# Attention with an expert layer: another order of the maxima's products, and loads issued at the start of a round

## The chip, the cores and the metric

One core of a Trainium2 chip. The metric is the device time of one execution in microseconds (us).

## What is computed

The reference, cut to the attention that the change touches (the expert layer that follows is not changed):

```
x = x + attention(layernorm(x), ctx, ctx)        # 4 batches, 1024 positions, 512 features
  qh = (q @ Wq.T), kh = (k @ Wk.T), vh = (v @ Wv.T + bv)     # 16 heads of 32
  scores = einsum('bhsd,bhtd->bhst', qh, kh) / sqrt(32)
  scores[mask: t >= s, except (0, 0)] = -inf
  probs = softmax(scores, axis=-1)
  out = einsum('bhst,bhtd->bhsd', probs, vh) @ Wo.T + bo
x = x + experts(layernorm(x))                     # 32 experts, 4 sets, tokens chosen by a maximum
```

## The kernel before

The kernel runs in three stages: the projections of 8 chunks of 512 positions (to about 290 us), the attention (to about 850 us), then output projection, routing and experts. Queries and keys are split in two parts each and stacked, so that one product over 96 rows is exact enough; a 97th row carries the negated maximum of each query.

The attention has 16 rounds (`NIT`, the variable `it`), one for each batch and group of four heads. The softmax needs the maximum of each query's scores before its exponentials. So there are two kinds of products on TensorE. The **maxima's products** (function `chunk`, line 1538) have queries on the partitions and keys in the columns; 48 of them make one round's maxima: 16 of `FIRST`, of 128 to 512 columns, for the first half of the queries, and 32 of `LATE`, 16 of them with the diagonal (128 to 512 columns) and 16 of 512 columns. The **scores** (function `score`, line 1559) have keys on the partitions; ScalarE turns them into exponentials (line 1450), and `values` and `sums` (lines 1578, 1592) multiply these with the values and add them up. While round `it` makes its scores, the maxima's products of round `it + 1` are put between them. Those of round 0 are put between the products of the projections of chunks 3 to 7, one in each of 48 places.

The twelve steps of a round (`STEPS`) go in six groups of two. TensorE's loop runs for each group: `full_width(it, g)`, then `values` and `sums` of the group. `full_width(it, g)` has eight slots; each ends with a score of the next group, and ahead of it stand as many maxima's products as `SHARE[g]` has for this slot. Which products they are, `FIRST` and then `LATE` say by their order. So three tables set the order on TensorE, and VectorE reads in the same order.

Maxima's products go into a ring of three PSUM banks (`MR = 3`, `reuse`): a product may start when VectorE has read the one three places back. VectorE reads a product with the diagonal by a custom instruction that also adds the mask (line 1313, followed by a readout of its accumulator), a full one by a reduction (line 1316). The scores have a ring of three banks of their own with ScalarE. When the 16 early maxima of the next round are read, TensorE transposes them (`turn`, line 1548, even numbers), ScalarE negates them (line 1428), SyncE copies them into the row of the query stack (`place_row`, line 1085); the 32 late ones follow in slot 2 of group 0 of the next round (odd numbers). A turn takes a place in the ring of three too. The early turn stands at the head of `full_width(it, EARLY_AT)`; `EARLY_AT` is one more than the first group by whose end 16 products have been made, here 2. The early row is needed by the first scores of the next round, made in `full_width(it, 5)`, the late row by those of `full_width(it, 1)`.

Between the products VectorE also inverts the sums of a half (`invert`, ahead of its products of groups 1 and 3), ScalarE copies outputs and sums out of PSUM (`take`), and GpSimd masks exponentials (lines 1193, 1197), adds up those of the full steps (`join`, line 1208, whose result the last `sums` of a round read) and multiplies outputs by the inverses (`divide`).

SyncE's queue has in each round: the late row, the store of the previous round's second half, the early row of the next round, a wait until four of this round's steps are done (`FETCH = 4`), the ten load DMAs of round `it + 2` (`load`: queries, keys, values, 3.5 MB), the store of this round's first half. The operands lie in three slots, so round `it + 2` takes those of round `it - 1`.

Of the kernel before, what the change touches and what calls it, by code (L numbers as in the profile page):

```python
# [19 lines left out]
NCH = T // CH  # L20
# [768 lines left out]
def project_attend_route(nc, a, m, keep):  # L789

    NIT = B * NG
# [6 lines left out]
    NS = len(STEPS)  # L798
    SPAN = [(max(CH * sh, P * j), CH * (sh + 1) - max(CH * sh, P * j)) for sh, j in STEPS]
    TOGETHER = [CH // w if w <= CH // 2 else 1 for _, w in SPAN]  # L800
    UNITS = [HG // n for n in TOGETHER]
    UNIT0 = [sum(UNITS[:k]) for k in range(NS + 1)]
    DIAG = [k for k, (sh, j) in enumerate(STEPS) if P * j >= CH * sh]

    FIRST = [(0, 0), (3, 1), (2, 2), (3, 2), (2, 1), (0, 2), (1, 3), (3, 0), (2, 0), (0, 1), (1, 0), (2, 3), (1, 1),
             (1, 2), (0, 3), (3, 3)]
    LATE = [(2, 5, 0), (1, 4, 1), (2, 7, 0), (0, 7, 0), (3, 5, 1), (3, 6, 1), (0, 5, 0), (3, 6, 0), (2, 7, 1),
# [3 lines left out]
    CHUNKS = [(h, i, 0, (i + 1) * P, True) for h, i in FIRST]  # L811
    EARLY = len(CHUNKS)
    for h, i, diag in LATE:
        CHUNKS.append((h, i, CH, (i + 1) * P - CH, True) if diag else (h, i, 0, CH, False))
    assert len(set(FIRST)) == HG * ST // 2 and len(set(LATE)) == HG * ST
    NC = len(CHUNKS)
# [6 lines left out]
    FULL = [k for k, (sh, j) in enumerate(STEPS) if P * j < CH * sh]  # L823
    JOINS = len(FULL) - 1
    FULL_AFTER = {6: 1, 8: 2, 10: 3}
    FETCH = 4

    INVERSIONS = {1: 1, 3: 0}
    TURN_SLOT = 2

    SHARE = [[1, 2, 0, 1, 1, 2, 1, 0], [0, 2, 0, 2, 1, 2, 1, 1], [4, 0, 1, 1, 1, 1, 0, 2], [1, 0, 0, 1, 0, 2, 2, 1],
             [1, 1, 0, 0, 1, 3, 0, 1], [2, 1, 0, 2, 1, 0, 0, 1]]

    def portions(g, chunks):
        return SHARE[g] if chunks else [0] * (2 * HG)

    PER = [sum(share) for share in SHARE]
    EARLY_AT = 1 + min(g for g in range(len(GROUPS)) if sum(PER[:g + 1]) >= EARLY)
# [14 lines left out]
    with ExitStack() as ctx:  # L853
# [6 lines left out]
        def sem(name):  # L860
            return ctx.enter_context(nc.semaphore(name))
# [101 lines left out]
        q_stored = sem("q_stored")  # L963
# [21 lines left out]
        step_done = sem("step_done")  # L985
# [55 lines left out]
        def fetch_q(eng, it, half, done):  # L1041

            b, g, slot = it // NG, it % NG, it % SLOTS
            for n, part in enumerate((m.q_hi, m.q_hi, m.q_lo)):
                src = part.rearrange("g (h p) (b s) -> b g p h s", p=HD, b=B)[b, g, :, :, half * CH:(half + 1) * CH]
                eng.dma_start(qs[slot][n * HD:(n + 1) * HD, half].bitcast(F32), src).then_inc(done, 16)

        def fetch_k(eng, it, cols, done):

            b, g, slot = it // NG, it % NG, it % SLOTS  # L1050
            for n, part in enumerate((m.k_hi, m.k_lo, m.k_hi)):
                src = part.rearrange("g (h p) (b s) -> b g p h s", p=HD, b=B)[b, g, :, :, cols]
                eng.dma_start(ks[slot][n * HD:(n + 1) * HD, :, cols].bitcast(F32), src).then_inc(done, 16)

        def fetch_v(eng, it):

            src = m.v.rearrange("(b t p) (g n) -> b g p t n", b=B, p=P, g=NG)[it // NG, it % NG]
            eng.dma_start(vt[it % SLOTS][:], src).then_inc(loaded[it % SLOTS], 16)

        def load(eng, it):  # L1060
            done = loaded[it % SLOTS]
            fetch_q(eng, it, 0, done)
            fetch_k(eng, it, slice(0, S), done)
            fetch_q(eng, it, 1, done)
            fetch_v(eng, it)

        with nc.Block() as block:
            @block.sync
            def _(sp):
# [7 lines left out]
                def store(it, half):  # L1077
                    sp.wait_ge(divided, it * 2 + half + 1)
                    sp.dma_start(m.o.rearrange("g p (b s) -> b g p s", b=B)[it // NG, it % NG][:, half * CH:(half + 1) * CH],
                                 o_n[:, half]).then_inc(o_stored[half], 16)  # L1080

                def place_row(turn):
                    it, late = turn // 2, turn % 2
                    sp.wait_ge(m_row_ready, turn + 1)
                    sp.dma_start(qs[it % SLOTS][R:R + 1, late].rearrange("p h s -> p (h s)").bitcast(F32),
                                 m_row[late][:].bitcast(F32)).then_inc(m_placed, 16)
# [60 lines left out]
                for it in range(NIT):  # L1147
                    place_row(2 * it + 1)
                    if it == NIT - 1:
                        sp.wait_ge(o_stored[0], 16 * it)  # L1150
                        sp.wait_ge(o_stored[1], 16 * (it - 1))
                        sp.wait_ge(step_done, it * NS)
                        sp.wait_ge(mx_read, NIT * NC)
                        router.sync_tiles(sp)
                    if it > 0:
                        store(it - 1, 1)
                    if it == NIT - 2:
                        sp.wait_ge(step_done, it * NS)
                        router.sync_weights(sp)
                    if it + 1 < NIT:  # L1160
                        place_row(2 * it + 2)
                    if it + 2 < NIT:
                        sp.wait_ge(step_done, it * NS + FETCH)
                        if it == 0:
                            sp.wait_ge(q_stored, 32 * NCH)
                        load(sp, it + 2)
                    store(it, 0)
                store(NIT - 1, 1)
                router.sync(sp)
# [528 lines left out]
def build(nc, a, m):  # L1698


    with ExitStack() as ctx:
        base = -(-nc.sbuf_base // 64) * 64
        sizes = (("pick", NE * T // P), ("x0", T), ("f1", 2 * NE * F), ("raw1", T), ("bias", E4), ("raw0", T), ("inner", E4 * NGR),
                 ("spare", T), ("wide", NE * NGR), ("x2_in", 3 * 4 * P), ("o_sum", 4 * 4 * P))
        keep = Plan()
        keep.at = {}
        for name, words in sizes:
            keep.at[name] = base
            base += words * 4

        def put(name, shape):
            return nc.alloc_sbuf_tensor_at("kept_" + name, shape, F32, offset=keep.at[name])

        keep.pick_tok = put("pick", [P, T // P, NE])
        keep.x0 = put("x0", [P, T // P, P])
        keep.f1 = put("f1", [P, 2, NE * F])
        keep.raw = [put("raw0", [P, T]), put("raw1", [P, T])]
        keep.bias = put("bias", [P, E4])
        keep.raw_in = ctx.enter_context(nc.semaphore("xn_raw_in"))
        keep.inner = put("inner", [P, E4, NGR])  # L1720
        keep.spare = put("spare", [P, T])
        keep.wide = put("wide", [P, NE * NGR])
        keep.x2_in = put("x2_in", [P, 3, 4, P])
        keep.o_sum = put("o_sum", [P, 4, 4, P])
        project_attend_route(nc, a, m, keep)
# [50 lines left out]
```

## Time and profile before

| | us |
|---|---|
| median of 3 runs | 1200.48 |
| lowest and highest | 1195.95, 1202.35 |
| the profiled execution, its time | 1198.24 |
| its span, first to last instruction | 1196.4 |

| engine | busy us | share of the span |
|---|---|---|
| TensorE, matmuls | 1140.7 | 95% |
| TensorE, weight loads | 781.5 | 65% |
| VectorE | 871.7 | 73% |
| ScalarE | 601.3 | 50% |
| GpSimd | 534.1 | 45% |

The mean granted clock of TensorE is 0.986. A matmul that has started counts as busy even while it waits for room behind another, and its end is modelled, so the busy share of TensorE alone doesn't show what it could save; the distances between starts in the timeline do. Rows below come from this execution; times in them are microseconds from the start of the span.

### The profile page before, as it was taken

To read this page: it belongs to the slowest core of one execution; us is meant where nothing else is said; L and a number is where in the kernel's file an instruction comes from. 1 tells how busy PE (TensorE), PEld (TensorE's weight loads), DVE (VectorE), ACT (ScalarE), POOL (GpSimd) and SP (SyncE) were. 2 spreads that over 40 slices of the span, in tenths; PEclk is the share of its full clock that TensorE was granted. 3 is DMA by queue.
4 is the path that set the end of the run, shared out by engine and by line. 5 is a ranking of instruction groups with operands and counts; after the bars stand their busy time and mean duration, and the time that the engine had idled before them with its cause. 6 is when DMAs were issued, how large, how long until landed. Compare 5 with 4: busy or idle time off the path is not lost. (4 is left out here: it accounts for less than half of the span.)

```text
span 1196.4 us, 29020 instructions
## 1 busy us (share of the span) xinstructions
PE 1140.7 (95%) x11456; PEld 781.5 (65%) x11456; DVE 871.7 (73%) x2202; ACT 601.3 (50%) x1108; POOL 534.1 (45%) x738
## 2 busy tenths in 40 slices
PE   7999999999999999999999999999999997888886
PEld 6787888887555555555555555554588886775664
DVE  7755777773777778777777877775488886766566
ACT  4322222223566666656666656667344444447674
POOL 1000000012666678776666877667765540001343
PEclk9999999999899999999999999999999999999898
DMA  8979887867554445665444566521499976754756
GB/s 290 337 254 300 276 316 247 305 207 227 133 118 108 106 105 132 142 142 125 104 109 103 129 142 141 131 87 63 135 331 296 315 249 184 227 163 133 216 166 174
DMA packets 179398, 223.44 MB, mean 187 GB/s; under 512 B 10176, under 2 KB 105920, under 8 KB 179264
## 3 DMA queue, kind: packets, MB, share of 16 engines
q1 hardware_dynamic: 179264, 221.62, 63.5%
q8 instruction: 89, 1.46, 0.5%
q14 instruction: 45, 0.37, 0.1%
HBM read 143.69 MB, written 77.63 MB: 185 GB/s over the span
## 5 line engine op out<-in xcount | busy, mean ns | idle before, releaser
L1450 ACT ACTIVATE p_t<-p_bank 128x512 f32<-128x512 f32 (+1 forms) x608 | 309.3, 577 | 163.3 <-PE p_bank L1559 161.3
L1313 DVE CUSTOM_DVE_ANT_0 tried<-p_bank,ban 128x128 bf16<-128x128 f32 (+3 forms) x512 | 231.4, 486 | 108.7 <-PE p_bank L1538 106.3
L1538 PE MATMUL p_bank<-k_stack,q_stack 96*128 96x512 f32 (+3 forms) x768 | 260.6, 380 | 0.4 <-DMA k_stack<-k_hi 0.2
L1559 PE MATMUL p_bank<-q_stack,k_stack 97*128 97x512 f32 (+3 forms) x768 | 233.9, 356 | 3.3 <-ACT p_t L1450 1.8
L1538 PEld LDWEIGHTS p_bank<-k_stack,q_stack 96*128 96x128 f32 x768 | 141.7, 189 | 107.4 <-issue 36.9
L1316 DVE TENSOR_REDUCE mx_ab<-p_bank 128x1 f32<-128x512 f32 x256 | 169.3, 686 | 3.2 <-PE p_bank L1538 0.2
L1197 POOL TENSOR_SCALAR_AFFINE_SELECT p_t<-p_t 128x128 f32<-128x128 f32 (+2 forms) x288 | 103.2, 361 | 145.8 <-ACT p_t L1450 139.3
L1578 PE MATMUL p_bank<-p_t,v_tile 128*32 128x512 f32 (+3 forms) x1536 | 164.6, 496 | 0.3 <-POOL p_t L1193 0.2
L1208 POOL TENSOR_TENSOR p_sum<-p_sum,p_t 128x512 f32<-128x512 f32 x128 | 160.2, 1283 | 0.0
L1559 PEld LDWEIGHTS p_bank<-q_stack,k_stack 97*128 97x128 f32 x768 | 137.2, 191 | 24.3 <-ACT p_t L1450 6.9
L561 POOL TENSOR_TENSOR kept_o_sum<-kept_o_sum,kept_x_in 128x512 f32<-128x512 f32 x30 | 38.3, 1281 | 173.4 <-ACT kept_o_sum L593 169.0
L636 DVE STREAM_TRANSPOSE y_rows<-kept_wide 128x1024 f32<-128x1024 f32 x64 | 73.0, 1208 | 38.6 <-ACT kept_wide L587 36.4
L1179 POOL MEMSET k_stack<- 1x4096 f32 x1 | 3.5, 3518 | 218.1 <-DVE c_lo L1381 218.1
L1592 PE MATMUL p_bank<-p_t,ones 128*32 128x512 f32 (+3 forms) x1024 | 94.6, 438 | 0.0
L1208 POOL TENSOR_TENSOR p_sum<-p_t 128x512 f32<-128x512 f32 x64 | 81.0, 1295 | 5.7 <-ACT p_t L1450 5.7
L1578 PEld LDWEIGHTS p_bank<-p_t,v_tile 128*32 128x32 f32 x1536 | 40.7, 110 | 65.0 <-issue 53.3
L587 ACT COPY kept_wide<-p_bank 128x1024 f32<-128x1024 f32 x64 | 61.7, 1028 | 18.2 <-PE p_bank L719 18.2
L1592 PEld LDWEIGHTS p_bank<-p_t,ones 128*32 128x32 f32 x1024 | 33.5, 111 | 38.0 <-issue 32.5
L1617 PE MATMUL p_bank<-c_hi,w_hi 128*128 128x512 f32 x128 | 52.1, 407 | 6.2 <-DVE wk_lo L1330 6.2
L351 PE MATMUL p_bank<-wo_hi,o_hi 128*128 128x512 f32 x128 | 55.3, 432 | 0.0
L603 ACT COPY kept_wide<-p_bank 128x1024 f32<-128x1024 f32 x32 | 34.9, 1112 | 38.0 <-PE p_bank L680 37.8
L1480 ACT CAST q_hi_s<-p_bank 128x512 fp32r<-128x512 f32 x32 | 18.7, 586 | 68.9 <-PE p_bank L1619 68.9
(135 smaller groups left out, 2096.6 us busy)
## 6 DMA issues: line engine op xcount, KB each, us to landing
q_stack<-q_hi SPq DMA_DIRECT2D x64, 256.0 KB, 6.3
k_stack<-k_hi SPq DMA_DIRECT2D x30, 512.0 KB, 9.8
kept_f<-in_f SPq DMA_DIRECT2D x20, 512.0 KB, 5.1
x_in<-in_x SPq DMA_DIRECT2D x8, 1024.0 KB, 9.9
x_t<-in_x_t SPq DMA_DIRECT2D x8, 1024.0 KB, 8.5
k_hi<-k_hi_s SPq DMA_DIRECT2D x8, 1024.0 KB, 5.7
k_lo<-k_lo_s SPq DMA_DIRECT2D x8, 1024.0 KB, 7.7
v_rows<-v_out SPq DMA_DIRECT2D x8, 1024.0 KB, 7.7
```

The costliest lines, as they stand in the source:

```text
L351: pe.matmul(bank[:, A + i % 2], oh, wo_hi[:, k], start=(k == 0), stop=False)
L587: act.copy(to, bank[:, n % RING * 2:n % RING * 2 + 2].rearrange("p q (m d) -> p d m q", m=2)).then_inc(kept_y, 1)
L636: ins = dve.transpose(y_rows[ch][:, :, d:d + ONCE].rearrange("p a d b -> p d a b"), y[u % 2][:, ch * P + d:ch * P + d + ONCE])
L1197: pool.affine_select(part, part, [[0, m], [1, P]], ALU.is_ge, 0.0, base=-1, channel_multiplier=-1).then_inc(masked, 1)
L1208: pool.tensor_tensor(p_sum[:, h], first, pt[:, FULL[n] % SLOTS_P, h], ALU.add).then_inc(joined, 1)
L1313: dve.tensor_tensor_reduce(scrap, got, ban0[:] if i == 0 else ban[:, CH - w:CH], 1.0, -3e38, ALU.add, ALU.max, to[:, col:col + 1]).then_in ...
L1316: dve.tensor_reduce(to[:, col:col + 1], got, AX.X, ALU.max).then_inc(mx_read, 1)
L1450: act.activation(pt[:, k % SLOTS_P, u * m:(u + 1) * m, 0:w], bank[:, SB + n % SR, 0:m * w].rearrange("p (m w) -> p m w", m=m), ACT.Exp, sc ...
L1538: pe.matmul(bank[:, to, 0:w], qs[it % SLOTS][0:R, i * P // CH, h, i * P % CH:i * P % CH + P], ks[it % SLOTS][0:R, h, t0:t0 + w], start=Tru ...
L1559: mm = pe.matmul(bank[:, SB + n % SR, h % m * w:(h % m + 1) * w], ks[slot][0:R + 1, h, j * P:(j + 1) * P], qs[slot][0:R + 1, sh, h, CH - w ...
L1578: mm = pe.matmul(bank[h * HD:(h + 1) * HD, OB, c0:c0 + w], vt[it % SLOTS][:, j, h * HD:(h + 1) * HD], pt[:, k % SLOTS_P, h, 0:w], start=(k ...
L1592: mm = pe.matmul(bank[h * HD:(h + 1) * HD, DB, c0:c0 + w], ones[:], of, start=(k in (0, 4)), stop=(k in (3, NS - 1)), tile_position=(0, h ...
```

## The change

The three tables are replaced by others of the same content: the same 16 and 32 products, in another order, and another split over the slots. Products per group go from 8, 9, 10, 7, 7, 7 to 6, 9, 9, 9, 7, 8. With them `EARLY_AT`, which is computed, goes from 2 to 3 (after two groups only 15 products have been made), and with it the early turn, ScalarE's negation and so the early row. On SyncE's queue the ten loads of round `it + 2` move from behind the early row to just behind the late row, ahead of the store of the previous second half and of the early row; they now wait for the end of the previous round's steps instead of four steps of this one. The rings (three banks each) are as they were.

```diff
-    FIRST = [(0, 0), (3, 1), (2, 2), (3, 2), (2, 1), (0, 2), (1, 3), (3, 0), (2, 0), (0, 1), (1, 0), (2, 3), (1, 1),
-             (1, 2), (0, 3), (3, 3)]
-    LATE = [(2, 5, 0), (1, 4, 1), (2, 7, 0), (0, 7, 0), (3, 5, 1), (3, 6, 1), (0, 5, 0), (3, 6, 0), (2, 7, 1),
-            (0, 6, 1), (2, 4, 0), (1, 6, 1), (1, 5, 0), (0, 5, 1), (2, 6, 1), (3, 4, 0), (0, 4, 0), (1, 6, 0),
-            (2, 5, 1), (3, 4, 1), (1, 5, 1), (3, 7, 0), (3, 7, 1), (2, 6, 0), (0, 7, 1), (0, 4, 1), (2, 4, 1),
-            (0, 6, 0), (1, 7, 0), (3, 5, 0), (1, 7, 1), (1, 4, 0)]
+    FIRST = [(1, 1), (0, 2), (1, 2), (2, 2), (2, 3), (2, 1), (0, 0), (3, 1), (1, 0), (0, 1), (2, 0), (3, 3), (1, 3),
+             (0, 3), (3, 2), (3, 0)]
+    LATE = [(0, 4, 1), (3, 6, 0), (2, 6, 1), (2, 6, 0), (2, 5, 0), (3, 7, 1), (2, 7, 0), (0, 4, 0), (1, 6, 1),
+            (1, 5, 1), (0, 6, 1), (3, 5, 1), (3, 6, 1), (0, 5, 1), (3, 5, 0), (2, 4, 0), (0, 5, 0), (2, 4, 1),
+            (2, 7, 1), (1, 4, 1), (1, 6, 0), (1, 7, 1), (0, 7, 0), (0, 7, 1), (3, 4, 1), (2, 5, 1), (3, 7, 0),
+            (0, 6, 0), (1, 5, 0), (3, 4, 0), (1, 4, 0), (1, 7, 0)]
...
-    FETCH = 4
...
-    SHARE = [[1, 2, 0, 1, 1, 2, 1, 0], [0, 2, 0, 2, 1, 2, 1, 1], [4, 0, 1, 1, 1, 1, 0, 2], [1, 0, 0, 1, 0, 2, 2, 1],
-             [1, 1, 0, 0, 1, 3, 0, 1], [2, 1, 0, 2, 1, 0, 0, 1]]
+    SHARE = [[1, 1, 1, 0, 1, 2, 0, 0], [0, 2, 1, 1, 2, 1, 1, 1], [3, 1, 1, 0, 1, 1, 1, 1], [1, 1, 0, 1, 1, 1, 2, 2],
+             [2, 0, 0, 0, 2, 0, 1, 2], [3, 0, 2, 1, 1, 0, 0, 1]]
...
+                    if it + 2 < NIT:
+                        if it == 0:
+                            sp.wait_ge(q_stored, 32 * NCH)
+                        else:
+                            sp.wait_ge(step_done, it * NS)
+                        load(sp, it + 2)
                     if it > 0:
                         store(it - 1, 1)
...
                         place_row(2 * it + 2)
-                    if it + 2 < NIT:
-                        sp.wait_ge(step_done, it * NS + FETCH)
-                        if it == 0:
-                            sp.wait_ge(q_stored, 32 * NCH)
-                        load(sp, it + 2)
                     store(it, 0)
```

An entry of `FIRST` is (head, block of queries i), of (i + 1) x 128 columns; one of `LATE` is (head, block, diagonal), of (i - 3) x 128 columns with the diagonal and 512 without.

## Rows read from the trace of the kernel before

**Rows 1.** Stretches of the attention: stretch, length, busy by engine, TensorE's clock, DMA share, GB/s.
```profile
526.00:535.00 9.00, 9.00 (x73) 4.73 (x72) 6.01 (x20) 4.40 (x9) 9.00 (x9) 1.00 1.07 239
535.00:540.00 5.00, 5.00 (x48) 2.90 (x48) 3.68 (x12) 3.65 (x8) 4.43 (x12) 1.00 0.02 9
```
**Rows 2.** Waits, whole span: engine, line, released by: us, times, longest.
```profile
PEld p_bank L1538 <- DVE mx_ab L1313: 21.4, 60, 0.8
...
PEld p_bank L1538 <- DVE mx_ab L1316: 17.0, 60, 0.4
```
**Rows 3.** VectorE's groups by form, 470 to 783 us: count, busy, mean ns.
```profile
L1316 DVE TENSOR_REDUCE mx_ab<-p_bank 128x1 f32<-128x512 f32 x144 | 95.0, 686 | 1.7
...
L1313 DVE CUSTOM_DVE_ANT_0 tried<-p_bank,ban 128x384 bf16<-128x384 f32 x72 | 39.9, 554 | 5.0 <-PE p_bank L1538 4.5
L1313 DVE CUSTOM_DVE_ANT_0 tried<-p_bank,ban 128x256 bf16<-128x256 f32 x73 | 30.7, 420 | 15.0 <-PE p_bank L1538 14.7
L1313 DVE CUSTOM_DVE_ANT_0 tried<-p_bank,ban 128x128 bf16<-128x128 f32 x73 | 20.5, 289 | 42.9 <-PE p_bank L1538 42.4
```
**Rows 4.** TensorE's timeline of one round: start, us, instruction.
```profile
504.00 0.33 PE L1538 MATMUL p_bank<-k_stack,q_stack 96*128 96x128 f32 x1
...
507.20 1.06 PE L1578 MATMUL p_bank<-p_t,v_tile 128*32 128x512 f32 x8
...
509.49 0.50 PE L1559 MATMUL p_bank<-q_stack,k_stack 97*128 97x512 f32 x1
...
513.42 0.85 PE L1578 MATMUL p_bank<-p_t,v_tile 128*32 128x384 f32 x8
...
515.71 0.28 PE L1548 MATMUL p_bank<-ident,mx_e 128*16 128x128 f32 x1
...
517.71 0.50 PE L1538 MATMUL p_bank<-k_stack,q_stack 96*128 96x512 f32 x1
518.05 0.34 PE L1559 MATMUL p_bank<-q_stack,k_stack 97*128 97x384 f32 x1
518.23 0.39 PE L1538 MATMUL p_bank<-k_stack,q_stack 96*128 96x512 f32 x1
518.46 0.39 PE L1559 MATMUL p_bank<-q_stack,k_stack 97*128 97x512 f32 x1
...
520.40 1.06 PE L1578 MATMUL p_bank<-p_t,v_tile 128*32 128x512 f32 x8
...
523.11 0.44 PE L1538 MATMUL p_bank<-k_stack,q_stack 96*128 96x384 f32 x1
...
526.42 0.85 PE L1578 MATMUL p_bank<-p_t,v_tile 128*32 128x384 f32 x8
...
528.71 0.39 PE L1538 MATMUL p_bank<-k_stack,q_stack 96*128 96x256 f32 x1
...
531.72 0.64 PE L1578 MATMUL p_bank<-p_t,v_tile 128*32 128x256 f32 x8
...
533.58 0.44 PE L1538 MATMUL p_bank<-k_stack,q_stack 96*128 96x128 f32 x2
...
536.51 0.43 PE L1578 MATMUL p_bank<-p_t,v_tile 128*32 128x128 f32 x8
...
538.80 0.33 PE L1538 MATMUL p_bank<-k_stack,q_stack 96*128 96x128 f32 x1
```
**Rows 5.** VectorE's timeline in stretch C of that round.
```profile
516.37 1.29 DVE L1316 TENSOR_REDUCE mx_ab<-p_bank 128x1 f32<-128x512 f32 x2
```
**Rows 6.** GpSimd's timeline, the last joins of that round.
```profile
532.15 5.03 POOL L1208 TENSOR_TENSOR p_sum<-p_sum,p_t 128x512 f32<-128x512 f32 x4
```
**Rows 7.** SyncE's timeline at the early row, and the landing of all 32 rows.
```profile
516.32 0.52 SPq L1085 DMA_DIRECT2D q_stack<-m_row  x1
...
DMA to landing us min/median/max: 1.8/1.8/10.0
```
**Rows 8.** TensorE's timeline in round 0, the first score that needs the late row.
```profile
297.96 0.50 PE L1559 MATMUL p_bank<-q_stack,k_stack 97*128 97x512 f32 x1 [1.58 <-DMA q_stack<-m_row]
```

## The prediction

> **What bounds the kernel now.** I first asked for the busy time by stretch of one steady round of the attention stage, because the change touches that stage alone. TensorE is busy for the whole of it at a granted clock of 1.00 [rows 1], so time can only come from gaps between its instructions that the record counts as busy. The waits say which: weight loads of the maxima's products (line 1538) stand behind VectorE's reads of earlier products (lines 1313 and 1316), 120 times in these two rows alone [rows 2]. Each product takes one of three PSUM buffers; the fourth has to wait until VectorE has read the first. VectorE's price of a read is 686, 554, 420 and 289 ns for 512, 384, 256 and 128 columns [rows 3], TensorE's only 0.23 us for 512 and 0.18 for 384 (518.23 to 518.46, 518.05 to 518.23 [rows 4]) and by the same timeline 0.12 and 0.11 for the narrower, so a burst of wide products overruns the three buffers.
>
> Then I read the steady round from 504.00 to 538.80, 34.80 us, in TensorE's timeline [rows 4]. It falls into six stretches of products and scores, A to F (calls 0 to 5 of full_width), with values and sums between. The stretches take 3.20, 3.93, 4.69, 3.31, 3.01 and 2.93 us, 21.07 in all; what lies between takes 2.29, 2.29, 2.71, 2.29, 1.86 and 2.29, 13.73 in all [rows 4]. The second sum has nothing that the change touches.
>
> **The price of a blocked product.** In stretch C a product of 512 columns is recorded at 517.71 and the next score at 518.05, 0.34 later; an unblocked pair (518.23, 518.46) is 0.23 apart [rows 4]. VectorE ended the read that it waited for at 516.37 + 1.29 = 517.66 [rows 5]. So the product in effect starts some 0.16 us after the read ends: its weights were not loaded ahead. My rule for a walk through a stretch: a product starts at the later of its own turn and 0.175 us after the end of the read three places back in the ring; VectorE starts a read 0.3 us (128 columns) to 0.49 us (512) after the product starts, or 0.08 before it ends the previous read, whose accumulator readout overlaps, so backlogged reads are 0.605, 0.475, 0.345 and 0.21 apart. A turn (transpose) takes a place in the ring too, free 0.58 us later, when ScalarE has negated it.
>
> **Part 1, the tables.** All 48 products, their widths and all scores stay, so TensorE's own time is the same; only the waits can change. Products per stretch go from 8, 9, 10, 7, 7, 7 to 6, 9, 9, 9, 7, 8. Two shapes change. First, narrow products now stand at the head of the bursts: B begins 128, 256, 128, 256, 128; C begins 128, 128. Their reads are short, so the buffers are free when the wide ones come. Second, the early row's turn (EARLY_AT) moves from the head of C, where a burst of four followed it, to the head of D, where single products are spread between scores.
>
> Stretch C as an example, time from its start. Three products (128, 128, 512) start at 0, 0.16 and 0.27 and find free buffers; reads end at 0.64, 0.85 and 1.46. The fourth (384) would start at 0.68 and waits for 0.64 + 0.175 = 0.815. The fifth and sixth (512) start unblocked at 1.17 and 1.84; the reads of the fourth to sixth end at 1.93, 2.54 and 3.14. The seventh and eighth start at 2.31 and 2.78, unblocked; the ninth would start at 3.25 and waits for 3.315. After it come a score and 0.33 to the values: 3.88 us. The same walk through C as it was gives 4.71, against 4.69 read [rows 4].
>
> In this way, before then after: A 3.19, 2.82; B 4.01, 3.65; C 4.71, 3.88; D 3.38, 3.76; E 3.05, 2.93; F 2.95, 3.38. D and F lose because they take in two products and one, and D ends in two pairs of 512. The walk of before sums to 21.29 against 21.07 read, so its error is 0.22 in six stretches and to the long side. The walk of after sums to 20.42. Read less walk is a gain of **0.65 us** a round, walk less walk 0.87; I take 0.75, nearer to the read end.
>
> What could take this back, and why I cost it at nothing. VectorE inverts the sums ahead of B and D (1.8 us). In the walk the last read of A ends at 3.4 and the inversion at 5.2, and B's first product can be read only from 5.4 on; the last read of C ends at 4.95, the inversion at 6.7, D's first read is due at 7.1. The cover is 0.2 and 0.4 us; without it B or D would lose what is missing. GpSimd's chain of joins ends at 532.15 + 5.03 = 537.18 [rows 6] and the sums that read it start in the middle of the last block at 537.8, 1.3 after 536.51 [rows 4]. From C's start to there were 22.1 us, and the walk again has 22.1 (C shorter, D and F longer), so the joins are not met earlier; the gain lies in A, B and C. ScalarE's negation for the early row leaves the head of C, where the copies of the outputs stood behind it, for the head of D, where it is followed by exponentials alone; nothing on that queue is due within its 0.3 us.
>
> **Part 2, the loads.** Each round has ten load DMAs on SyncE's queue for the round after next. Before, they were issued behind the early row's DMA, at 516.9 (0.6 after it), and kept the DMA engines busy until about 535: the share is 1.07 up to 535 and 0.02 after it [rows 1, 7]. That is 18 us, ended 4 us before the products that need them in the next round. No product of a steady round waits for a load, so issuing them earlier gains **nothing**. The wait that they stand behind, the end of the previous round's steps, is over when the late row has been placed. Moved behind them on SyncE are the store of the previous second half (its output is due only after 5 us of issues, and its buffer is needed a round later) and the early row, whose turn comes in D. Late row: it is still ahead of the loads. It lands 1.8 us after its issue [rows 7], some 2 us before B, and A is now 0.4 shorter; 1.6 us are left. Early row: see the first rival. Cost zero in the forecast; bound below, nothing, since no load is waited for.
>
> **First round.** Its late row stood behind the last projection stores, and TensorE waited 1.58 us for it until 297.96 [rows 8]. What A saves there is lost in that wait. So 14 rounds count in full (0.75 each, 10.5 us) and the first with 0.75 - 0.38 = 0.4. The last round has no products. Iteration 0's products, made during the projections, only change order between long projection products there, each of which gives VectorE more time than a read takes: zero, with 1 us either way.
>
> **Sum.** 1198.24 - 10.9 = 1187.3 us against the profiled execution's own time (span 1196.4). The median of the runs is 2.24 above that execution: **1189.6 us**. With 0.45 to 1.05 a round the forecast's own range is 1185 to 1194.
>
> **Rivals.** (a) Slower: the early row behind the loads. In the walk the loads start 2.4 us after A and, by the 18 us above, end at 20.5; the early row's turn is at D's start, 17.6, its DMA 0.6 later at 18.2 [rows 4, 7]. So it is now queued while loads are still moving, where before it was ahead of them. F needs it, at 28.5. If it comes in 1.8 us it lands at 20.0; if it takes the 10.0 us that is the longest landing of such a row [rows 7], it lands at 28.2, just in time. It decides from a landing of 10.3 us on; at 11.5 us it costs 1.2 us in 15 rounds, 18 us, which with the gain gives 1207. Against it: 8 us of spare, and the loads' own speed. Chance 0.07, with 0.03 more for other ways to lose over 6 us. The Trainium skill (DMA: Bandwidth & Descriptors, section Queues, rings and completion order) says that a DMA's semaphore increment lands only after every earlier write of the same DMA engine; by that the row lands no earlier than the loads ahead of it, at some 20.5. That still is ahead of F and leaves the sum as it is, but it is the reason that I give (a) more than a token chance. No row of before shows a row queued behind loads.
>
> (b) No change: the waits come back in D and F. If nine and eight products there lose what C lost with ten (0.9 us of waits against the 0.6 and 0.3 that I walked), 0.3 + 0.6 = 0.9 us a round is given back, and the time is about 1200. For it: D starts wide and ends in two pairs. Against: C lost most by the turn ahead of a burst of four and by reads of 512 columns queued in a row, which D and F have less of. Chance 0.15.
>
> (c) A larger gain. If the walk is too long after as before, by 0.22, and two of the small blocks that I counted (0.03 to 0.07 each) don't occur, 1.05 to 1.2 us a round are saved: 1181 to 1184. Chance 0.08.
>
> The forecast has 0.67. The range reaches over (b) and most of (c): 1182 to 1203, leaving out (a) and the ends. About 0.5% (6 us) is what a measurement of this kernel can tell from no change. Faster by more than that: most of the forecast and (c), 0.73; the same, (b) and the forecast's weak end, 0.17; slower 0.10.
>
> **What the profile after would show.** A steady round of about 34.05 us; A to F near 2.8, 3.6, 3.9, 3.7, 2.9, 3.3; the blocks between them unchanged at 13.7. No blocked burst at the head of C. The early row's DMA issued 0.6 us after D starts, with a landing of 2 to 4 us; the late row unchanged at 1.8. No wait of TensorE for a load or a row outside the first round. The prediction is wrong if D and F exceed 4 us, if VectorE's inversion delays B or D, if the joins hold the last sums, or if F starts with a wait for the row.

## The result

| | us |
|---|---|
| before, median of 4 runs | 1199.97 |
| changed, median of 4 runs (1185.73 to 1188.89) | 1187.26 |
| ratio, with its 95% interval | 0.9898 (0.9867 to 0.9928) |
| profiled execution of the changed kernel: time, span | 1185.73, 1184.0 |

The changed kernel is faster by 12.7 us, 1.0% by the ratio; 1189.6 had been forecast. The same matmuls and reads are done. From the changed kernel's page, busy time and granted clock in 40 slices:

```profile
PE 1123.2 (95%) x11456; PEld 778.2 (66%) x11456; DVE 865.8 (73%) x2202; ACT 602.3 (51%) x1108; POOL 534.6 (45%) x738
...
PEclk9999999999999999999999999999999999999998
```

TensorE has the same 11456 matmuls and 17.5 us less busy time: time between starts that counted as busy is gone, some 3 us of it time at a lower clock (below). The two waits of [rows 2] are now

```profile
PEld p_bank L1538 <- DVE mx_ab L1313: 22.6, 75, 0.8
...
PEld p_bank L1538 <- DVE mx_ab L1316: 12.0, 45, 0.3
```

as many as before (120), but 34.6 us instead of 38.4. These two rows alone show 3.8 us. The weight loads of the maxima's products wait for the ring in two more rows, for the reads of the early products (`mx_e`) and for ScalarE's negation of the turn (`m_row`). Before:

```profile
PEld p_bank L1538 <- DVE mx_e L1313: 10.8, 44, 0.4
...
PEld p_bank L1538 <- ACT m_row L1428: 4.8, 15, 0.3
```

After, the second row is gone:

```profile
PEld p_bank L1538 <- DVE mx_e L1313: 9.0, 30, 1.1
```

All rows together are 54.0 us before and 43.6 after, 10.4 us less, and rounds 1 to 14 together are 10.0 us shorter. The clearest reading is the timeline of one steady round, the starts of its six stretches A to F and of the blocks behind them, to be held against [rows 4]:

```profile
497.09 0.39 PE L1538 MATMUL p_bank<-k_stack,q_stack 96*128 96x256 f32 x1
...
499.89 1.07 PE L1578 MATMUL p_bank<-p_t,v_tile 128*32 128x512 f32 x8
...
502.18 0.50 PE L1559 MATMUL p_bank<-q_stack,k_stack 97*128 97x512 f32 x1
...
505.75 0.85 PE L1578 MATMUL p_bank<-p_t,v_tile 128*32 128x384 f32 x8
...
508.04 0.72 PE L1538 MATMUL p_bank<-k_stack,q_stack 96*128 96x128 f32 x3
...
511.93 1.06 PE L1578 MATMUL p_bank<-p_t,v_tile 128*32 128x512 f32 x8
...
514.64 0.28 PE L1548 MATMUL p_bank<-ident,mx_e 128*16 128x128 f32 x1
...
518.42 0.85 PE L1578 MATMUL p_bank<-p_t,v_tile 128*32 128x384 f32 x8
...
520.70 0.61 PE L1538 MATMUL p_bank<-k_stack,q_stack 96*128 96x128 f32 x2
...
523.67 0.64 PE L1578 MATMUL p_bank<-p_t,v_tile 128*32 128x256 f32 x8
...
525.53 0.73 PE L1538 MATMUL p_bank<-k_stack,q_stack 96*128 96x128 f32 x3
...
528.88 0.43 PE L1578 MATMUL p_bank<-p_t,v_tile 128*32 128x128 f32 x8
...
531.16 0.39 PE L1538 MATMUL p_bank<-k_stack,q_stack 96*128 96x256 f32 x1
```

| stretch | A | B | C | D | E | F | sum | round |
|---|---|---|---|---|---|---|---|---|
| before, read | 3.20 | 3.93 | 4.69 | 3.31 | 3.01 | 2.93 | 21.07 | 34.80 |
| after, walked in the prediction | 2.82 | 3.65 | 3.88 | 3.76 | 2.93 | 3.38 | 20.42 | 34.15 |
| after, read | 2.80 | 3.57 | 3.89 | 3.78 | 2.97 | 3.35 | 20.36 | 34.07 |

The blocks between the stretches are the same within 0.01 us: 2.29, 2.29, 2.71, 2.28, 1.86 and 2.28. This round is 0.73 us shorter; in the mean of rounds 1 to 14 it is 0.72 (34.78 to 34.06).

SyncE's queue in that round, and the early row's time to landing (a window with that row alone), to hold against [rows 7]:

```profile
498.74 0.52 SPq L1084 DMA_DIRECT2D q_stack<-m_row  x1
499.30 1.05 SPq L1045 DMA_DIRECT2D q_stack<-q_hi  x2
...
515.25 0.51 SPq L1084 DMA_DIRECT2D q_stack<-m_row  x1
...
DMA to landing us min/median/max: 3.9/3.9/3.9
```

The DMA share from 499 to 517, and from 519 on:

```profile
499.00:517.00 18.00, 18.00 (x143) 10.40 (x141) 15.14 (x54) 12.30 (x27) 10.65 (x19) 1.00 0.96 209
519.00:530.00 11.00, 11.00 (x99) 6.51 (x95) 8.29 (x23) 5.45 (x11) 11.00 (x15) 1.00 0.07 25
```

The loads now fill the first half of the round. The early row comes in at their tail and lands after 3.9 us, 6.4 us ahead of F. Over rounds 0 to 13 it takes 3.7 to 5.0 us, so at least 5.3 us are to spare.

One thing in the two profiles is not the change. In round 0 of the profiled execution of before, the granted clock stood at 0.5 (1.2 GHz) from 299.0 to 305.8 us; in that of after it did not. The same stretch, before and then after:

```profile
299.00:306.00 7.00, 7.00 (x29) 4.15 (x31) 4.14 (x15) 4.06 (x8) 1.17 (x4) 0.51 0.00 0
```
```profile
299.00:306.00 7.00, 7.00 (x56) 4.46 (x55) 5.24 (x24) 5.84 (x13) 1.75 (x6) 1.00 1.04 234
```

So the 12.4 us between the two spans are made up of 10.0 in rounds 1 to 14, 3.2 in round 0 (2.8 of them this clock, the rest the tables) and 0.2 ahead of it, less 1.0 us by which the part from round 15 on is longer. That last part was not looked into. Both kernels wait 1.6 us for the late row there [rows 8], and over the executions of all kernels with that wait the clock fell in some and not in others (below).

### The profile page after: what moved, and what is told of

Read it like the earlier page. It is cut to its first block and busy times, and to the rows that moved or that the text cites. A ratio compares the mean times of both kernels' runs of the same rounds, so it can differ in the third digit from the quotient of the medians.

```text
span 1184.0 us, 29018 instructions
## 1 busy us (share of the span) xinstructions
PE 1123.2 (95%) x11456; PEld 778.2 (66%) x11456; DVE 865.8 (73%) x2202; ACT 602.3 (51%) x1108; POOL 534.6 (45%) x738
## 5 line engine op out<-in xcount | busy, mean ns | idle before, releaser
L1450 ACT ACTIVATE p_t<-p_bank 128x512 f32<-128x512 f32 (+1 forms) x608 | 305.7, 584 | 129.4 <-PE p_bank L1559 123.0
L1313 DVE CUSTOM_DVE_ANT_0 tried<-p_bank,ban 128x256 bf16<-128x256 f32 (+3 forms) x512 | 229.4, 487 | 104.4 <-PE p_bank L1538 103.3
L1538 PE MATMUL p_bank<-k_stack,q_stack 96*128 96x512 f32 (+3 forms) x768 | 256.9, 375 | 0.8 <-DVE mx_e L1313 0.7
L1538 PEld LDWEIGHTS p_bank<-k_stack,q_stack 96*128 96x128 f32 x768 | 137.5, 188 | 89.1 <-issue 30.5
L1316 DVE TENSOR_REDUCE mx_ab<-p_bank 128x1 f32<-128x512 f32 x256 | 163.6, 683 | 0.0
L561 POOL TENSOR_TENSOR kept_o_sum<-kept_o_sum,kept_x_in 128x512 f32<-128x512 f32 x30 | 38.4, 1283 | 174.4 <-ACT kept_o_sum L593 169.9
```

The costliest lines, as they stand in the source:

```text
L1313: dve.tensor_tensor_reduce(scrap, got, ban0[:] if i == 0 else ban[:, CH - w:CH], 1.0, -3e38, ALU.add, ALU.max, to[:, col:col + 1]).then_in ...
L1316: dve.tensor_reduce(to[:, col:col + 1], got, AX.X, ALU.max).then_inc(mx_read, 1)
L1450: act.activation(pt[:, k % SLOTS_P, u * m:(u + 1) * m, 0:w], bank[:, SB + n % SR, 0:m * w].rearrange("p (m w) -> p m w", m=m), ACT.Exp, sc ...
L1538: pe.matmul(bank[:, to, 0:w], qs[it % SLOTS][0:R, i * P // CH, h, i * P % CH:i * P % CH + P], ks[it % SLOTS][0:R, h, t0:t0 + w], start=Tru ...
```

## The experiments

**1. The tables alone.** Loads where they were:

```diff
--- changed kernel
+++ tables alone
+    FETCH = 4
...
-                    if it + 2 < NIT:
-                        if it == 0:
-                            sp.wait_ge(q_stored, 32 * NCH)
-                        else:
-                            sp.wait_ge(step_done, it * NS)
-                        load(sp, it + 2)
                     if it > 0:
                         store(it - 1, 1)
...
                         place_row(2 * it + 2)
+                    if it + 2 < NIT:
+                        sp.wait_ge(step_done, it * NS + FETCH)
+                        if it == 0:
+                            sp.wait_ge(q_stored, 32 * NCH)
+                        load(sp, it + 2)
```

> The new tables, the loads where they were before. Theory (fewer blocked products, loads without effect): a steady round of 34.05 to 34.10 us, stretches A to F 2.79, 3.57, 3.88, 3.77, 2.97, 3.36 as in the changed kernel, time within 3 us of it (1185 to 1190). Rival (part of the gain comes from the moved loads, whose traffic now falls on other stretches): a round of 34.3 us or more and 1190 to 1195.

Measured: 1269.74 us, ratio 1.0586 (1.0532 to 1.0639). Neither theory: the tables alone make the kernel 5.9% slower. Stretches B to F are those of the changed kernel (3.57, 3.88, 3.77, 2.97, 3.36), so the tables do what they did, but the end of a round does not. Its waits, SyncE's queue in one round, and the first product of the next:

```profile
PEld p_bank L1538 <- DMA v_tile<-v_rows: 59.9, 14, 4.9
PE p_bank L1538 <- DMA v_tile<-v_rows: 47.2, 14, 4.0
```
```profile
549.35 0.51 SPq L1085 DMA_DIRECT2D q_stack<-m_row  x1
549.91 1.05 SPq L1046 DMA_DIRECT2D q_stack<-q_hi  x2
...
554.45 0.43 SPq L1058 DMA_DIRECT2D v_tile<-v_rows  x1
```
```profile
569.32 0.58 PE L1538 MATMUL p_bank<-k_stack,q_stack 96*128 96x256 f32 x1 [3.97 <-DMA v_tile<-v_rows]
```
```profile
568.00:572.00 4.00, 2.69 (x9) 2.50 (x10) 1.56 (x6) 1.38 (x4) 0.59 (x2) 0.65 0.08 28
```

The early turn went from the head of C to that of D, one stretch and one block later, 3.9 + 2.7 = 6.6 us. The loads stand on SyncE behind the early row, so they went with it, from 4 us of spare to about 2.6 us too late. (The last load of before lands at 535.5, 3.3 us ahead of the round at 538.80; by this spare it is 3.3 us too late.) The first product of stretch A waits 2.9 to 4.0 us in each of 14 rounds, 3.4 in the mean. The granted clock falls around the end of the wait (0.65 in the last row above, the stretch from 568 to 572), so that A itself takes 3.6 to 4.5 us instead of 2.8 and the block behind it up to 4.2 instead of 2.29. Rounds 1 to 13 are 39.7 us in the mean, 5.6 more than in the changed kernel.

**2. The loads alone.** The changed kernel with `FIRST`, `LATE` and `SHARE` of before.

> The old tables, the loads at the start of a round. Theory: a steady round of 34.77 us as before, time 1197 to 1202. Rival (the loads carry part of the gain): 34.5 us a round or less, 1195 or less; rival (they cost, and the tables hide it): 35 us, 1204.

Measured: 1201.02 us, ratio 1.0005 (0.9983 to 1.0026), rounds of 34.75 to 34.83. With the old tables the moved loads do nothing, as predicted. In this kernel the early row (turn still at C) is queued with more of the loads in front of it, and its landings are 7.6 to 11.3 us in rounds 0 to 13; its first user, F, never waits.

**3 and 4. Short reads.** How much of the difference is VectorE's reads? Here VectorE reads only 128 columns of each product, which leaves most maxima incomplete; TensorE's products are all there.

```diff
-                    got = bank[:, RINGS["chunk", n][0], 0:w]
+                    got = bank[:, RINGS["chunk", n][0], 0:P]
...
-                        dve.tensor_tensor_reduce(scrap, got, ban0[:] if i == 0 else ban[:, CH - w:CH],
+                        dve.tensor_tensor_reduce(scrap, got, ban0[:] if i == 0 else ban[:, CH - w:CH - w + P],
```

> The kernel before, but VectorE reads only the first 128 columns of each of the maxima's products, so most maxima are left incomplete; TensorE's products are all there. No read is then long enough to block the ring. Theory (same work on TensorE, the difference is VectorE's reads blocking products): the six stretches sum to 18.8 to 19.1 us, a round of 32.5 to 32.8, and the two tables come within 0.15 us of each other. Rival (the order itself matters to TensorE, by which weight load stands behind which matmul): the old tables stay 0.4 us or more above the new ones.

> The changed kernel with the same short reads (128 columns of each product, most maxima incomplete). Theory: 18.8 to 19.1 us for the six stretches, within 0.15 us of the old tables with short reads. Rival: 0.4 us or more below them.

| | A | B | C | D | E | F | sum |
|---|---|---|---|---|---|---|---|
| old tables, short reads | 2.85 | 3.68 | 4.22 | 3.03 | 2.86 | 2.93 | 19.57 |
| new tables, short reads | 2.62 | 3.57 | 3.77 | 3.22 | 3.00 | 3.15 | 19.33 |

With short reads both are faster than either kernel (1179.57 and 1178.54 us, one execution each), and the difference between the tables in A to F shrinks from 0.71 to 0.24. So 0.47 of the 0.71 us are VectorE's reads blocking products. That is less than my theory had (within 0.15), and less than 0.4 remains, so the rival falls too: a third of the gain is something else. Both sums are also above the 18.8 to 19.1 that I had expected. In the new tables 20.34 - 19.33 = 1.0 us a round is still lost to reads. Whole rounds are 0.33 apart (33.37 and 33.04), because the block behind F takes 2.36 us instead of 2.29 in the old tables with short reads. The two times are only 1.0 us apart since the clock fell in round 0 of the second execution (below).

The table also shows what is no gain: with short reads C is 0.45 us shorter in the new tables, B 0.11 and A 0.23, and D, E and F are 0.19, 0.14 and 0.22 longer. This is TensorE's own work moved from one stretch to another: C's products have 29 blocks of 128 columns instead of 33, those of D 27 instead of 24 and those of F 27 instead of 22.

**5. The order alone, and 6. the split alone.** The kernel before with the new `FIRST` and `LATE` only, and with the new `SHARE` only.

> The kernel before with the new FIRST and LATE, but the old SHARE (8, 9, 10, 7, 7, 7). Theory, by the walk: stretch C would have nine wide products and one of 256 columns queued: 5.3 us against 4.69, and the round about 35.3, slower than before. Rival (narrow products at the head of bursts are what gains, whatever the split): a round of 34.4 or less.

> The kernel before with the new SHARE (6, 9, 9, 9, 7, 8, and with it the early turn at D), but the old FIRST and LATE. Theory, by the walk: C about 4.3 us and D about 4.3 (five reads of 384 or 512 columns among its first six), the round 34.9 to 35.2, no gain. Rival (the split and the moved turn carry the gain): 34.3 or less.

The order alone: 1231.87 us, a round of 36.65, C 5.37 (5.3 walked). TensorE's timeline at the head of its C, and the end:

```profile
600.45 0.28 PE L1548 MATMUL p_bank<-ident,mx_e 128*16 128x128 f32 x1
600.48 1.11 PE L1538 MATMUL p_bank<-k_stack,q_stack 96*128 96x512 f32 x3
601.74 0.50 PE L1538 MATMUL p_bank<-k_stack,q_stack 96*128 96x512 f32 x1 [0.15 <-DVE mx_ab L1316]
...
605.82 1.06 PE L1578 MATMUL p_bank<-p_t,v_tile 128*32 128x512 f32 x8
```

Four wide products at the head of a burst of four: the fourth starts 1.3 us after the turn. With the old split the narrow products of the new order fall in other places, A takes 3.8, B 4.1 and E 3.4 us. That I had walked C alone is why 35.3 was too low for the round. The split alone: C 4.53 and D 4.46 us where 4.3 and 4.3 were walked, A to F 22.5 us in the rounds in which the clock did not fall in A, 1.5 more than before. Even without the late loads that is a round of 36.2 us, where 34.9 to 35.2 was expected, since E and F, which I had not walked, take 3.24 and 3.67 us. Its time, 1266.97 us, has the late loads of experiment 1 as well. Neither half gains: each table is made for the other.

**7. The early turn at D,** in the kernel before, and **9.** the same with short reads and with the loads moved.

```diff
-    EARLY_AT = 1 + min(g for g in range(len(GROUPS)) if sum(PER[:g + 1]) >= EARLY)
+    EARLY_AT = 3
```

> The kernel before with the early row's turn at the head of D instead of C, tables as before. My prediction named the turn ahead of a burst of four as a main loss of C. Theory of the prediction: C falls by about 0.3 us, to 4.4. Rival, from the walk done again without the turn: the third product starts 0.34 sooner, but the fifth then waits for the same read of VectorE (until 1.5 us from the start), so C stays within 0.1 us of 4.69.

Measured: C 4.67 us (4.69 before), the rival's value. The late loads show here too, 1303.51 us. The fourth product of C starts 0.72 us after its head instead of 0.98, the fifth 1.39 instead of 1.45, and from there on they follow as before. The weight loads' waits say the same: the 4.8 us for the negation are gone, and the waits for reads grow from 49.2 to 52.3 us.

> The old tables with short reads (128 columns of each product, most maxima incomplete) and the loads at the start of a round, and the early row's turn moved from the head of C to that of D. With short reads the old tables stayed 0.25 us above the new ones (19.57 against 19.32 us for A to F). Theory: that rest is the turn ahead of a burst of four, whose place in the ring comes free only after the negation, and which long reads hid: C falls from 4.22 to 3.9 and the sum to 19.25. Rival (the rest lies in the order itself): C stays at 4.2, the sum at 19.5 or more.

With short reads the turn does cost. The heads and ends of C, old tables with short reads first, then the same with the turn at D:

```profile
571.44 0.28 PE L1548 MATMUL p_bank<-ident,mx_e 128*16 128x128 f32 x1
571.48 1.22 PE L1538 MATMUL p_bank<-k_stack,q_stack 96*128 96x128 f32 x4
...
575.66 1.07 PE L1578 MATMUL p_bank<-p_t,v_tile 128*32 128x512 f32 x8
```
```profile
569.58 1.10 PE L1538 MATMUL p_bank<-k_stack,q_stack 96*128 96x128 f32 x4
...
573.67 1.07 PE L1578 MATMUL p_bank<-p_t,v_tile 128*32 128x512 f32 x8
```

4.22 against 4.09 us, less than half of what the theory had (3.9); the sum is 19.43 instead of 19.57. So of the 0.24 us between the tables with short reads, 0.14 is the turn ahead of the burst, and 0.1 stays unexplained.

**8. Loads ahead of the early row.** This gives the price of the first rival.

```diff
-                    if it + 2 < NIT:
-                        if it == 0:
-                            sp.wait_ge(q_stored, 32 * NCH)
-                        else:
-                            sp.wait_ge(step_done, it * NS)
-                        load(sp, it + 2)
                     if it > 0:
                         store(it - 1, 1)
+                    if it + 2 < NIT:
+                        if it == 0:
+                            sp.wait_ge(q_stored, 32 * NCH)
+                        sp.wait_ge(step_done, it * NS + 4)
+                        load(sp, it + 2)
```

> The changed kernel with the ten loads issued after four of the round's steps (at the head of C) but ahead of the early row, so that the row (at the head of D, 6.6 us later) has 11 us of loads still in front of it. Theory (a row waits for the loads ahead of it on its rings): its landing is 11 to 13 us, F starts with a wait of 1 to 2.5 us in each round, 15 to 35 us in all. Rival (a row of 8 KB passes by the loads): landing 4 us or less, a round of 34.07 us as in the changed kernel.

Measured: 1212.51 us in one execution, 25 more than the changed kernel. The landing of one early row, and TensorE's waits for rows in all:

```profile
DMA to landing us min/median/max: 12.2/12.2/12.2
```
```profile
PEld p_bank L1558 <- DMA q_stack<-m_row: 17.6, 13, 1.9
PE p_bank L1558 <- DMA q_stack<-m_row: 13.5, 13, 1.6
```

The 14 early rows of rounds 0 to 13 land after 11.5 to 12.6 us, and F takes 4.1 to 4.9 us in 13 of these rounds (3.36 without a wait), 1.2 us more in the mean. That makes some 17 of the 25 us. Some 6 more are two falls of the granted clock to 0.5: in round 0, and in round 8 behind its wait for the row, where F takes 6.67 us and the block behind it 3.84. An 8 KB row does not pass the loads: in the round shown in the changed kernel, in experiment 2 and here the last load lands at 518.3, 522.5 and 537.9 us, and the early row at 519.1, 523.3 and 538.1.

**10. The row first, 11. the changed kernel again,** on one chip. In round 0 the late row is issued ahead of the last two query stores:

```diff
+                    if c + 1 < NCH:
                         sp.dma_start(by_chunk["q_hi"][c], q_hi[:].bitcast(F32)).then_inc(q_stored, 16)
                         sp.dma_start(by_chunk["q_lo"][c], q_lo[:].bitcast(F32)).then_inc(q_stored, 16)
...
                     place_row(2 * it + 1)
+                    if it == 0:
+                        sp.dma_start(by_chunk["q_hi"][NCH - 1], q_hi[:].bitcast(F32)).then_inc(q_stored, 16)
+                        sp.dma_start(by_chunk["q_lo"][NCH - 1], q_lo[:].bitcast(F32)).then_inc(q_stored, 16)
```

> The changed kernel, but in round 0 the late row is issued ahead of the last chunk's two query stores instead of behind them. Theory (the row waits for the 2 MB ahead of it, 6.9 us to landing, and TensorE for the row, 1.6 us): landing 1.8 to 2.5 us, no wait of TensorE for the row, so 1.6 us less in every execution, and no fall of the granted clock in round 0, which cost 3 us in the executions that had it: 1183 to 1186, ratio to the changed kernel 0.996 to 0.999. Rival (the row was late for another reason): 1187 as the changed kernel.

> The changed kernel once more, on the same chip as the run with the row first. Theory: a round of 34.07 us again and 1185 to 1190 us; whether the clock falls in round 0 is left to the execution, as stretch B of round 0 had 3.6 to 4.1 us in six executions of variants and 5.2 to 5.7 in four.

| | median | runs | ratio to before |
|---|---|---|---|
| row first | 1185.64 | 1185.09 to 1186.21 (4) | 0.9875 (0.9853 to 0.9896) |
| changed kernel | 1190.04 | 1186.43 to 1196.37 (6) | 0.9922 (0.9896 to 0.9948) |

The row's landing in round 0 and the first score that needs it, with the row first:

```profile
DMA to landing us min/median/max: 1.8/1.8/1.8
```
```profile
296.88 0.50 PE L1563 MATMUL p_bank<-q_stack,k_stack 97*128 97x512 f32 x1
```

1.8 us instead of 6.9, and no wait. Round 1 begins at 326.1 instead of 327.4 (changed kernel again), so 1.3 us are seen. F of round 0 gives 0.2 back (3.57 instead of 3.35). Its early row shows why: the loads of round 0 wait for the query stores, which are now later, and the row behind them takes 11.0 us to land. It lands at 320.9 us, and the score that needs it starts at 320.99. The median is within the 1183 to 1186 that were expected. All four runs lie below all six of the changed kernel on this chip, but the first comparison of the changed kernel had one of 1185.73, inside its range. It is the fastest version of the study; that it is faster by more than the 1.3 us of the profile is not shown. The clock did not fall in round 0 of either profiled execution, so what the second half of the expectation said of it is untested.

## Why the prediction was right, and where it was not

**What bounds the kernel: right.** Time came from nothing but the distances between starts in the stretches, and shorter reads alone take 1.5 us a round off the old tables (21.04 to 19.57) and 1.0 off the new.

**The walk: right.** Its largest miss in one stretch is 0.08 us (B), the sum is 0.06 too long. The two stretches that were to lose did (D 3.78 for 3.76, F 3.35 for 3.38). Of the two values of the gain, read less walk gave 0.65 and walk less walk 0.87; I took 0.75, and the rounds show 0.72. For tables that I had not walked in full (5 and 6), the stretches that I did walk came within 0.25 us; of those that I left out, A moved by 0.6 us in experiment 5 and F by 0.7 in experiment 6.

**What would show it:** the blocks are unchanged; inversions and joins hold nothing up (B is shorter than walked, the block behind F is 2.28); the early row is issued 0.6 us after D's head and lands after 3.7 to 5.0 us, which in nine of 14 rounds is above the 2 to 4 forecast and costs nothing. A round of about 34.05 was forecast, 34.06 came.

**The sum: right.** Of the 10.9 us forecast, the profiles show 10.0 in rounds 1 to 14 (10.5 forecast) and 0.3 in round 0 apart from the clock (0.4 forecast). The medians differ by 12.7 in the first comparison and by 10.4 in the second (experiment 11), so how near a median comes to the forecast is chance within some 2 us. No fall of the clock was in the sum. One time in the prediction does not follow from its own numbers: 1.05 to 1.2 us a round, the larger gain, make 1183 to 1185 us and not 1181 to 1184.

**The reason given second for the tables failed:** that the turn's move away from the burst in C gains. Experiment 7 shows 0.02 us. The walk done again without it says why: the third product starts sooner (by 0.34 us in the walk, 0.18 in the trace), and then the fifth waits for the same read until nearly the same time. Two waits in series on one chain of reads are not a sum. What C gained is its products: one less, and the narrow ones first. Of its 0.80 us, 0.45 are there with short reads too (work that D, E and F take over, and the turn); the rest is reads. Only where reads are short is the turn worth 0.13 us.

**The price of the moved loads failed as a reason, though not as a term.** The step was "no product of a steady round waits for a load, so issuing them earlier gains nothing". True of the kernel before (experiment 2), and in the sum of both parts together the term is zero as well. But I costed the second part against the old tables and not against the first part. Having written that the early row moves to D, and that the loads were issued behind it, with 4 us of spare, I had both numbers for what the tables alone would do: 6.6 us later with 4 us of spare (3.3 by the landing of the last load). The loads' move is what the tables need; without it they cost 69 us instead of gaining 13.

**Round 0.** I took its late row's wait as it was, and this was so (1.56 us). The fall of the clock behind it I did not mention. In the profiled executions of ten kernels with that wait, before and after among them, stretch B of round 0 took 3.6 to 4.1 us in six and 5.2 to 5.7 in four, old and new tables, loads moved or not, on both sides; runs 9 and 11, with the wait too, had 3.69 and 3.58. A comparison of two profiles alone would have put these 3 us down to the change. The Trainium skill (TensorE: Matmul & The Clock Gate, section What's actually happening) says that activity releases a throttle which is the default state; experiment 1 agrees, with a granted clock of 0.65 over 568 to 572 us after a wait of 4 us.

**The first rival** was worked out rightly in its mechanism, and its bound is 0.5 us off. I had it decide from a landing of 10.3 us on, when F starts; but products stand ahead of F's first score. In the trace a landing of 11.0 us costs 0.2 (experiment 10), 11.5 costs 0.7 to 0.8 and 12.2 costs 1.4 to 1.5 (experiment 8), where I had 1.2 for 11.5. With the loads 9 us later (experiment 8) the waits for the row cost some 17 us, where the prediction had 18, and the kernel is 25 us slower with the falls of the clock. The rule of the Trainium skill on increments that land after earlier writes of the same DMA engine, cited in the prediction (DMA: Bandwidth & Descriptors, Queues, rings and completion order), agrees with the trace: the row lands 0.2 to 0.8 us behind the last load in the three rounds read (after 3.7 to 5.0, 7.6 to 11.3 and 11.5 to 12.6 us in the three kernels, by how much of them is ahead). The changed kernel has 5.3 us of spare or more. The second rival did not come: D and F took what was walked.

## What to carry to other kernels

A ring that blocks can be walked: own time per product, end of the read so many places back, and the price of a weight load that is not hidden. The error was 0.3% of the six stretches after the change and 1.0% before it. Where a table moves one step, list what is queued behind that step on every queue and compare its spare time with the shift, before costing the next edit; two edits that are each worth nothing or less may be one change. Put the operations that free a buffer quickly at the head of a burst and the turn of the ring that takes long away from it, and check by the chain whether the second matters.

## What was not expected of the hardware

A wait of TensorE of 1.6 us is followed by a fall of the granted clock to 0.5 for 6.8 us in some executions of a kernel and not in others; the price is about 3 us here (stretch B of round 0 at 5.7 us instead of 3.9, and the block behind it at 3.33 instead of 2.29). In experiment 6, after waits of TensorE of 1.7 to 3.0 us ahead of A, it fell in 7 of 14 rounds; in experiment 1, after 2.9 to 4.0 us, in all 14. A small DMA of 8 KB issued behind 2 MB of stores took 6.9 us to land, and 1.8 us when issued ahead of them.
